# One pipeline of 64 turns in place of four stages, with the feed-forward in bursts inside the attention steps

## What is computed

```python
x = x + attention(layernorm(x), Wq, bq, Wk, bk, Wv, bv, Wo)      # scale 8**-0.5, corners of the scores set to -1e9
x = x + ffn(layernorm(x))
x = x + attention_b(layernorm(x), w_qkv, w_out)                  # no bias, scores / sqrt(128)
x = x + ffn(layernorm(x))

def ffn(x):
    gate = softmax(x.mean(axis=1) @ gate_w.T)                    # one gate vector per item
    top_w, top_i = top_k(gate, 2)
    top_w = top_w / (top_w.sum(-1) + 1e-8)
    h = gelu(einsum('bsd,bkcd->bksc', x, down_w[top_i]) + down_b[top_i]) * top_w
    return einsum('bksc,bkdc->bsd', h, up_w[top_i]) + (top_w * up_b[top_i]).sum(1)

```

## Time and profile before

| | |
|---|---|
| median of three runs | 1039.13 us (1038.06 to 1042.84) |
| the profiled execution | 1037.22 us |
| its span, first to last instruction | 1035.4 us |
| mean granted clock of TensorE | 0.968 |
| busy: PE, DVE, ACT, POOL | 88%, 76%, 73%, 57% |
| DMA | 131.64 MB, 127 GB/s |

### The profile page before, as it was taken

How to read it: one execution, slowest core, us unless ns; L and a number is a source line. 1 busy time by engine, 2 the same in 40 slices (tenths; PEclk the granted TensorE clock), 3 DMA queues, 4 the chain that set the end, 5 groups by cost and what they waited for, 6 DMA issues and landing times. The chain is left out here.

```text
span 1035.4 us, 27550 instructions
## 1 busy us (share of the span) xinstructions
PE 910.3 (88%) x10204; PEld 518.6 (50%) x10204; DVE 788.7 (76%) x1398; ACT 759.7 (73%) x1324; POOL 593.3 (57%) x1011
## 2 busy tenths in 40 slices
PE   1479999999999999984876999999999999998577
PEld 1235555555555555442653555555555555554266
DVE  0378888888888888843449898899999999885244
ACT  1147888888888888783753788888888888888566
POOL 4555666666666666423256566666666666643211
PEclk9989999999999999997997999999999999999889
DMA  8544545445554545300035444445544445440023
GB/s 235 173 147 146 145 145 147 145 147 145 145 148 145 145 146 147 113 3 21 2 103 161 154 148 149 150 144 150 149 154 147 145 144 152 148 130 3 1 60 105
DMA packets 140516, 131.64 MB, mean 127 GB/s; under 512 B 9880, under 2 KB 121888, under 8 KB 140256
## 3 DMA queue, kind: packets, MB, share of 16 engines
q1 hardware_dynamic: 139312, 128.49, 41.9%
q10 hardware_dynamic: 1072, 1.40, 0.5%
HBM read 73.75 MB, written 55.57 MB: 125 GB/s over the span
## 5 line engine op out<-in xcount | busy, mean ns | idle before, releaser
L379 DVE TENSOR_REDUCE nmax<-ring 128x4 f32<-128x1024 f32 x512 | 607.7, 1218 | 73.0 <-PE ring L504 73.0
L418 ACT ACTIVATE probs<-ring 128x1024 f32<-128x1024 f32 x512 | 509.1, 1024 | 78.8 <-PE ring L521 75.4
L486 PE MATMUL values_bank<-probs,values 128*32 128x256 f32 x4096 | 274.8, 386 | 5.8 <-ACT probs L418 5.8
L504 PE MATMUL ring<-k_stack,q_stack 64*128 64x256 bf16 x2048 | 201.2, 278 | 44.2 <-DMA k_stack<-scratch 20.4
L335 POOL TENSOR_SCALAR xy<-x,mv,rstd 128x128 f32<-128x128 f32 x256 | 201.1, 795 | 8.7
L521 PE MATMUL ring<-q_stack,k_stack 64*128 64x256 bf16 x2048 | 187.3, 273 | 0.4 <-DVE nmax L379 0.2
L486 PEld LDWEIGHTS values_bank<-probs,values 128*32 128x32 f32 x4096 | 107.0, 109 | 90.8 <-issue 24.0
L298 POOL TENSOR_SCALAR mparts<-nmax 128x32 bf16<-128x32 f32 x64 | 13.8, 216 | 231.7 <-DVE nmax L379 231.7
L504 PEld LDWEIGHTS ring<-k_stack,q_stack 64*128 64x128 bf16 x2048 | 75.6, 95 | 138.9 <-ACT probs L418 67.3
L521 PEld LDWEIGHTS ring<-q_stack,k_stack 64*128 64x128 bf16 x2048 | 83.8, 95 | 74.7 <-issue 37.8
L304 POOL TENSOR_TENSOR parts<-rest,parts 128x512 bf16<-128x512 f32 x64 | 74.1, 1158 | 5.4
(11 more groups left out here) (99 smaller groups left out, 1027.0 us busy)
## 6 DMA issues: line engine op xcount, KB each, us to landing
q_stack<-scratch SPq DMA_DIRECT2D x128, 256.0 KB
k_stack<-scratch SPq DMA_DIRECT2D x128, 256.0 KB
scratch<-parts SPq DMA_DIRECT2D x128, 192.0 KB, 2.3
scratch<-parts SPq DMA_DIRECT2D x128, 128.0 KB, 2.2
scratch<-parts SPq DMA_DIRECT2D x128, 64.0 KB, 3.1
out<-x SPq DMA_DIRECT2D x32, 128.0 KB, 1.8
q_stack<-maxT SPq DMA_DIRECT2D x128, 12.0 KB
scratch<-in_tail SPq DMA_DIRECT2D x8, 128.0 KB, 3.8
```

Source lines behind the costliest of these rows:

```text
L379: nc.vector.tensor_reduce(dst, src, axis=AX.X, op=ALU.max, negate=True).then_inc(max_done, 1)
L418: nc.scalar.activation(probs[g % 2][:, c:c + 2, :, :], pair_of_exps(n, p)[:, :, :].rearrange("p x (k q) -> p x k q", k=TILES), ACT.Exp).th ...
L486: last = nc.tensor.matmul(values_bank[32 * c:32 * (c + 1), a * TOKENS:(a + 1) * TOKENS], values[item % RING][:, k, PER_GROUP * g + c, :], ...
L504: last = nc.tensor.matmul(pair_of_scores(n, p)[:, a, t * TOKENS:(t + 1) * TOKENS], q_stack[z][rows, p, t * P:(t + 1) * P], k_stack[z][rows ...
```

## The change

The four stages and the blocks between them go. One pipeline runs over 64 turns, two per item: turn t is attention a of item t for t < 32, and attention b of item t - 32 from there. Steps run from n = -6 to 70. The feed-forward is done in 16 groups of four turns, each as a burst in one step (`BURSTS`): four first products (`down`) behind pair 4's scores, four Gelus on ACT behind the Exp of pair 3, the biases and second products (`up`) behind pair 4's Exp scores, two additions to x on DVE at position 5. The two products take a buffer each in the rotation of `ring`, which is now counted by a list of uses. Gating is done in ten batches of eight or four turns, each in three successive steps: logits, then weights and transposes, then biases, all in `m_bank` ahead of the value projection. DVE makes it, with ACT for Exp and the copies, and POOL for the split of the biases.

POOL copies both down weights of an item (`prepare`). Both halves of the scaled up weights are made by DVE at position 4, with one item in each of the four steps ahead of a burst for the first ten groups, two in each of the last two steps for the next four, and four in the step ahead for the last two. Gelu and Exp alternate on ACT, and no table is preloaded. The attention step's order on PE is changed: the value projection stands behind pair 4's scores, group 1's weighting behind pair 5's Exp scores, and the Exp scores of pair 6 behind the norm's transposes; ACT's copies of the values and of the norms move ahead by one position. In the opening nothing waits for a whole block: x is loaded in six pieces, of which four are issued in early steps, PE waits for three early weights, and POOL zeroes some more tiles. Results are stored two items at a time, one step behind their burst, in the second half.

```diff
-CHUNKS = ((0, 2), (2, 9), (9, ITEMS))
+CHUNKS = ((0, 2), (2, 9), (9, 15), (15, 21), (21, 27), (27, ITEMS))
+RING = 4
+TURNS = 2 * ITEMS
+GROUP = 4
+DEEP = 2 * GROUP
...
+        def sync_opening(sp):
+            load_x(sp, 0)
+            constant_rows(sp, 0)
+            load_x(sp, 1)
...
+            for dst, src in early:
+                act.dma_start(dst, src).then_inc(early_in, 16)
+            for dst, src in loads:
+                act.dma_start(dst, src).then_inc(consts_in, 16)
+            act.wait_ge(early_in, 16 * EARLY_LOADS)
+            nc.scalar.copy(identb[:, :], ident[:, :])
+            nc.scalar.mul(bqs[:, :], wa[:, 512:513], float(HEAD) ** -0.5)
+            nc.scalar.mul(wa[:, 0:WIDTH], wa[:, 0:WIDTH], float(HEAD) ** -0.5)
+            nc.scalar.mul(wb[:, 0:WIDTH], wb[:, 0:WIDTH], float(WIDTH) ** -0.5).then_inc(weights_ready, 1)
+            act.wait_ge(weights_ready, 1)
...
+        FIRST, LAST = -6, 70
+        BATCHES = ((0, 8), (8, 8), (16, 8), (24, 8), (32, 8), (40, 8), (48, 4), (52, 4), (56, 4), (60, 4))
+        LATE, FIRST_BY_VECTOR = 56, 0
+        BURSTS = (17, 21, 25, 29, 33, 37, 41, 45, 49, 53, 55, 57, 59, 63, 66, 70)
+        DOWN_AFTER, UP_AFTER = 3, 4
+        MIXING = 12
+        WHICH, NBEST = 3, 4
+        SPLITS = 5
+        PREPARED = {}
+        for group, burst in enumerate(BURSTS):
+            for j in range(GROUP):
+                turn = group * GROUP + j
+                early_step = burst - (1 if turn >= LATE else GROUP - j if turn < 40 else 2 - j // 2)
+                PREPARED.setdefault(early_step, []).append(turn)
...
+        def fill_pair(pe, *use):
+
+            if place[use] < 3:
+                return
+            kind, of, p = uses[place[use] - 3]
+            if kind == "scores":
+                pe.wait_ge(max_done, of * PAIRS + p + 1)
+            elif kind == "exps":
+                pe.wait_ge(exp_done, of * PAIRS + p + 1)
+            elif kind == "down":
+                pe.wait_ge(h_ready, (of + 1) * GROUP)
+            else:
+                pe.wait_ge(added, (of + 1) * 2)
...
+                    b = batch_at(n, 1)
+                    if b is not None:
+
+                        rows = BATCHES[b][1]
+                        sp.wait_ge(mixing, MIXING * b + WHICH)
+                        if before_batch(b):
+                            sp.wait_ge(wd_ready, before_batch(b))
+                            sp.wait_ge(wu_ready, before_batch(b))
+                        sp.dma_start(index[b % 2][0:1, 0:rows * TOP], which[0:rows, 0:TOP]).then_inc(index_in, 16)
+                    group = group_at(n - 1) if n <= LAST else None
+                    if group is not None and group * GROUP >= ITEMS:
+                        store(sp, group)
...
+                def prepare(turn):
+
+                    b, z, group = batch_of(turn), turn % DEEP, turn // GROUP
+                    if group not in experts:
+                        experts[group] = experts_of(group, pool)
+                    if turn >= DEEP:
+                        pool.wait_ge(up_done, (turn - DEEP) // 2 + 1)
+                    for k in range(TOP):
+                        last = nc.gpsimd.tensor_copy(wd[z][:, k:k + 1, :], down_sb[:, bass.ds(experts[group][TOP * (turn % GROUP) + k], 1), :])
+                    last.then_inc(wd_ready, 1)
...
+                def split_biases(b):
+
+                    parts_b, mid_rows, lo_rows = biasu_parts[b % 2], slice(ITEMS, 2 * ITEMS), slice(2 * ITEMS, 3 * ITEMS)
+                    pool.wait_ge(biases_ready, b + 1)
+                    if before_batch(b):
+                        pool.wait_ge(up_done, before_batch(b) // 2)
...
+                    if p == 3:
+                        for turn in PREPARED.get(n, ()):
+                            prepare(turn)
...
+                def best_of(b):
+
+                    rows = slice(0, BATCHES[b][1])
+                    dve.wait_ge(logits_done, b + 1)
+                    link(nc.vector.tensor_scalar(logit[rows, :], m_bank[rows, 0:EXPERTS], 1.0 / TOKENS, None, ALU.mult))
+                    link(nc.vector.max(best[rows, :], logit[rows, :]))
+                    if b > 0:
+                        dve.wait_ge(index_in, 16 * b)
...
+                    if p == 0 and batch_at(n, 1) is not None:
+                        weights_of(batch_at(n, 1))
...
+                    if p == 2 and batch_at(n, 1) is not None:
+                        spread(batch_at(n, 1))
...
+                    if p == 4 and batch_at(n, 0) is not None:
+                        best_of(batch_at(n, 0))
...
+                    if p == 5 and group_at(n) is not None:
+
+                        group = group_at(n)
+                        for half in range(2):
+                            dve.wait_ge(up_done, 2 * group + half + 1)
+                            xs = x[:, tiles_of(group * GROUP + 2 * half, 2), :]
+                            src = pair_of("up", group, 0)[:, half, :].rearrange("p (t d) -> p t d", d=WIDTH)
+                            nc.vector.tensor_tensor(xs, xs, src, ALU.add).then_inc(added, 1)
...
+                    if p == 4:
+                        for turn in PREPARED.get(n, ()):
+                            if turn >= FIRST_BY_VECTOR:
+                                if turn % GROUP == 0:
+                                    experts[0] = experts_of(turn // GROUP, dve)
+                                dve.wait_ge(weight_ready, batch_of(turn) + 1)
+                                if turn >= DEEP:
+                                    dve.wait_ge(up_done, (turn - DEEP) // 2 + 1)
+                                z, col = turn % DEEP, turn - BATCHES[batch_of(turn)][0]
+                                for k in range(TOP):
+                                    half = slice(HIDDEN * k, HIDDEN * (k + 1))
+                                    last = nc.vector.tensor_scalar(wu[z][half, :].unsqueeze(1),
+                                                                   up_sb[half, bass.ds(experts[0][TOP * (turn % GROUP) + k], 1), :],
+                                                                   weight[batch_of(turn) % 2][half, col:col + 1], None, ALU.mult)
+                                last.then_inc(wu_ready, 1)
...
+                    if p == 3 and group_at(n) is not None:
+
+                        group = group_at(n)
+                        act.wait_ge(biases_ready, batch_of(group * GROUP) + 1)
+                        for j in range(GROUP):
+                            turn = group * GROUP + j
+                            run, col = batch_of(turn) % 2, turn - BATCHES[batch_of(turn)][0]
+                            act.wait_ge(down_done, group * GROUP + 2 * (j // 2) + 2)
+                            if group > 0:
+                                act.wait_ge(up_done, 2 * (group - 1) + j // 2 + 1)
+                            src = pair_of("down", group, 0)[:, j // 2, (j % 2) * TOKENS:(j % 2 + 1) * TOKENS]
+                            nc.scalar.activation(hT[j][:, :], src, ACT.Gelu, bias=biasd[run][:, col:col + 1]).then_inc(h_ready, 1)
+                    if p == 3 and batch_at(n, 1) is not None:
+
+                        b = batch_at(n, 1)
+                        act.wait_ge(mixed_done, b + 1)
+                        if before_batch(b):
+                            act.wait_ge(wu_ready, before_batch(b))
+                        nc.scalar.copy(weight[b % 2][:, :], m_bank[:, 0:ITEMS])
+                        nc.scalar.copy(hotT[:, :, :].rearrange("p a b -> p (a b)"), m_bank[0:TOP * EXPERTS, ITEMS:5 * ITEMS]).then_inc(weight_ready, 1)
...
+                def down(group):
+
+                    fill_pair(pe, "down", group, 0)
+                    pe.wait_ge(wd_ready, (group + 1) * GROUP)
+                    bank = pair_of("down", group, 0)
+                    for j in range(GROUP):
+                        turn = group * GROUP + j
+                        nc.tensor.matmul(bank[:, j // 2, (j % 2) * TOKENS:(j % 2 + 1) * TOKENS],
+                                         wd[turn % DEEP][:, :, :].rearrange("p a b -> p (a b)"), normT[:, turn % ITEMS, :],
+                                         start=(j % 2 == 0), stop=(j % 2 == 1), skip_group_check=True).then_inc(down_done, 1)
...
+                def up(group):
+
+                    b = batch_of(group * GROUP)
+                    fill_pair(pe, "up", group, 0)
+                    pe.wait_ge(split_done, SPLITS * (b + 1))
+                    pe.wait_ge(wu_ready, (group + 1) * GROUP)
...
+                def mixes(b):
+
+                    fill_m(pe, weight_ready, b + 1)
+                    pe.wait_ge(mixing, MIXING * (b + 1))
+                    nc.tensor.transpose(m_bank[:, 0:ITEMS], wide[:, :, :].rearrange("p a b -> p (a b)"), ident[0:ITEMS, 0:ITEMS])
+                    for k in range(4):
+                        src = (hot if k == 0 else mix)[:, :, :].rearrange("p a b -> p (a b)")
```

(29 more changed lines are left out.)

1015 lines of the change are left out of this document (475 added, 540 removed).

## The result

The change makes the kernel slower: 1070.46 us, median of four executions (1069.75 to 1070.99), against 1038.6 us for the kernel before beside it. The ratio is 1.030, with an interval from 1.027 to 1.033. The forecast was 1022 us, with a range from 988 to 1056. The profiled execution took 1069.75 us. Its span is 1067.9 us, where the sum gave 1018.0, so 49.9 us have to be found.

The account below looks back on a forecast made before the run. PE's work and an equally long DVE-POOL-PE loop were taken to bound the 12.93 us step. Terms: 77.5 + 798.5 + 58.5 + 6.5 + 18 + 30 + 29 = 1018.0 us of span, forecast 1022 us, range 988 to 1056.

Parts of the forecast that it names:

- products: Scaled second weights made on DVE inside the steps: 18 us together, between 5 and 46.
- gating: Ten batches inside the attention steps, each over three successive steps: 30 us, between 18 and 48.
- 13 bursts: Feed-forward bursts in full steps: 4.5 us each, between 4.3 and 7.1, 58.5 us for thirteen.
- old work and step 63: Middle: 32 steady steps and the whole second stage, 798.5 us, plus the burst beside eight Exps, 6.5 us.
- The frame: First to last addition: 63 intervals, old work alone 798.5 us, steady step 12.93; PE's new order taken at nothing.
- Rival (c): Slower by the port or DVE loop: every product waits for POOL, 28 us more, 1050 us; chance 0.12.
- The expert numbers: DVE's load of eight per group: some 2 us, 0.85 beyond the reduction that it runs beside.
- the load at 6.43: Opening of the kernel before: ACT's 1.28 us table load ran ahead of a wait; bursts were taken to do likewise.
- Rival (b): Slower by table switches: both loads of every burst on the path, 7.1 us a burst, 1055 us; chance 0.15.
- rival (d): No difference: gating is 6 us a batch instead of 3.75, 1040 us; chance 0.14.
- Ends: First addition at 77.5, between 73 and 80; part after the last addition 29 us, between 25 and 36.
- rival (a): Nearly everything hides, steps follow PE's bare work: gating 18, preparation 5, bursts 4.3 each, about 988 us; chance 0.17.

Follow-up runs that it names:

- second kernel: The changed kernel with POOL instead of DVE making all scaled second weights: 1027.18 us, 1025.4 of span.
- e5_early_table: The changed kernel with products on POOL, plus the Gelu table load put by hand behind the Exp of pair 3: 1005.0 us of span.
- e9_read_first: e5_early_table plus DVE reading the logits ahead of the reduction of pair 4: 999.5 us of span; timed 1002.5 us, ratio 0.966.
- e10_table_alone: The changed kernel, products still on DVE, plus only the early Gelu table load: 1049.7 us of span.
- e11_early_timed: The same kernel as e5_early_table, timed over four executions: 1007.98 us, ratio 0.972 to the kernel before.
- e4_wait_order: The changed kernel with the two waits ahead of each Gelu in swapped order: 1066.2 us of span.

## Why the prediction was wrong

The second kernel gives the ledger of the middle: 913.6 us between first and last addition without products on DVE, 877.9 with one batch of gating, of which that batch is 6.5.

| term between first and last addition | forecast | measured | from |
|---|---|---|---|
| products | 18 | 46.7 | 960.3 - 913.6 |
| gating | 30 | 42.2 | 913.6 - 877.9, and the batch that stays |
| 13 bursts | 58.5 | 67.2 | 13 x (18.14 - 12.97) |
| old work and step 63 | 805.0 | 804.2 | the rest |
| sum | 911.5 | 960.3 | |

The ledger has no row for the clock, and the forecast of the middle had no term for it either. The changed kernel's middle has eight steps with a lower granted clock, each 1.2 to 1.6 us longer than the like step without, some 11 us together; the second kernel's has six, some 9 us; the two attention stages of the kernel before have none (granted clock 1.00 in both). So about 9 of the 42.2 us, and 2 or 3 of the 46.7, are clock. Without them gating is 33 us and the products about 44.

**The frame held.** 63 intervals of old work at the old period, the new order on PE at nothing: plain steps went from 12.93 to 12.97, and the rest of the ledger is within 1 us. That whatever stands between pair 4 and pair 7 on DVE lengthens the step held too, and it made the error below expensive.

**The products: wrong by 28.7 us, the step that failed.** I took "four of 17 were longer, by 0.6 us together" as the rate at which a product meets POOL. But that rate belonged to the place where the products stood, not to the operation. In the old feed-forward 4 of all 64 products were longer. At position 4 of a step without a burst POOL is in the split of queries and keys, L501 to L510. There a pair takes up to 1.88 us, not 0.58; in burst steps, where it comes later, it takes 0.58 (296.73). The trace of the kernel before showed this place already: in the step of the earlier trace rows, while DVE reduces pairs 4 and 5 from 199.51 on, POOL is in the same split.

```profile
200.10 0.62 POOL L302 TENSOR_SCALAR parts<-rest 128x512 bf16<-128x512 f32 x1
200.80 1.16 POOL L304 TENSOR_TENSOR parts<-rest,parts 128x512 bf16<-128x512 f32 x1
```

A product behind the reduction of pair 4 would have started near 200.7, beside these. The two-port lock that the Trainium skill states (SBUF — State Buffer, Who interferes with whom) would have said this; I named it, noted that by it most products would be delayed, and took the other value. The trace agrees with the rule in three ways: 564 ns in the mean with POOL beside about half of the products, 285 away from it, and statistics, which show no delay, at 286 in the same place. Rival (c) had the right cause, and its sum of 46 is close to the measured 46.7, but that is partly luck. It gave each of 104 products 0.31 us more, 32 us. In the trace 60 of the 128 products are long, by 0.6 us each in the mean (36 us), and the other 68 are not; 2 or 3 of the 46.7 are clock. Where a pair takes 1.2 to 1.3 us more, all of it passes to the step, but for the steps right behind a burst, which are only 0.8 to 0.9 longer. The forecast also counted the pairs beside gating and in bursts as free: those with logits cost 0.8 to 0.9 us of step, those in bursts without biases 0.7.

**The expert numbers: too small, and hidden.** I estimated 2 us for eight numbers. In the burst step 1.77 us of idle time stand behind the reduction of pair 4, which takes 1.23: 3 us in all, an estimate that takes the loads to start with the reduction, which no row shows. PE is in the first products meanwhile, and DVE's idle time before pair 5 was foreseen. As the burst step is the same without products but for 0.7 us (18.86 against 18.14), this cost is small.

**Bursts: wrong by 8.7 us.** The forecast rested on the load at 6.43, which ran ahead of a wait. In the bursts it runs behind the wait for the first products. The row at 6.43 stood in an opening where the load is the first thing that the block does, and it did not tell where a load goes once an operation of the other table stands before it. The text priced the other case at 1.1 us for PE; 1.15 was measured. Of the 5.17 us, 1.19 are this and 3.98 are the rest: so the product work itself was cheaper than my 4.3, of which 0.1 for two changes of form was an estimate that no run shows by itself. Rival (b), with both loads on the path and 7.1 us a burst, was wrong: the load back to Exp is hidden. The drain of 1380 ns that the Trainium skill gives beside each load (ScalarE: Activation LUTs, What ACT_TABLE_LOAD costs) is not seen here: the load at 294.84 ends at 296.12 and the Gelu starts at 296.13, the load at 298.06 starts 0.02 us after the copy before it has ended, and removing the loads after the early placement is worth 2.6 us of span, less than 0.1 per switch.

**Gating: wrong by 12.2 us, of which 9 are the clock.** Over eight batches, as the forecast and rival (d) count them, that is 5.3 us a batch, where I had 3.75 and rival (d) had 6; at the full clock it is 4.1. Logits cost 1.78 as against 1.4, the transposes 1.4 to 1.5 against 1.1, biases in a burst step 1.3 against 1.7. What I missed in the transposes is DVE: the small operations that build the one-hot rows stand ahead of pair 3 and of the scaled output `o`, and PE waits up to 1.3 us for `o` (L854, 7.4 us in nine waits). The clock drops of these two kernels all come in steps with transposes or biases (last section). The biases in a burst step wait for the Gelus and the table (L918 for `biasu`, 10.8 us in seven waits; 4.2 us once the load is early). I had foreseen this order, at 0.7 us.

**Ends.** First addition 2.4 us later than forecast, last part 1.2 us shorter. The last burst shows a term that was mis-sized there:

```profile
1057.14 2.88 DVE L648 TENSOR_SCALAR wu<-up_sb,weight 64x128 f32 x8 [3.08 <-issue]
...
1057.46 3.75 PE L812 MATMUL ring<-normT,wd 128*128 128x256 f32 x8 [1.11 <-POOL wd L428]
```

1.0 us was forecast for the first products beside the table load; the eight matmuls take 3.75 here, where the granted clock is 0.50, and 1.99 in the burst at 293.62. Shorter chains elsewhere in the end made up for it.

**What the prediction asked to look at.** Burst steps of 18.86 against a limit of 18.8, products of 564 ns instead of 270 to 300, and a table load that stands behind 1.35 us of idle time instead of right behind the operation before it, with nothing wrong in plain steps: so it pointed to the bursts and the products at once. The range failed because it was built from cases of which one is wrong at a time. Here three terms were off in the same direction (28.7 + 12.2 + 8.7 us), and they had something in common: each was taken from rows of a place where little ran beside the operation, and used for a place where much does. The sum of rival (a) was also slightly off: its terms give 983 us of span, which is 986.5 and not 988; this changes nothing here.

## What to carry to other kernels

A duration taken from a trace belongs to the place in which it was measured; before moving an operation, look at what the other engines run at its new place, POOL above all for a scale or copy on DVE. Where two functions alternate on ACT and the second one waits for a matmul, put its table load by hand ahead of that wait. Price the whole chain of a one-bank resource by who reads it: a read that stands behind a 1.2 us reduction costs PE that reduction. And before two single runs are compared by their totals, compare the granted clock step by step.

## What the runs showed of the hardware

**A DVE product beside POOL's split ends when a POOL instruction ends.** The row at 517.28 holds two products. The first takes 0.63 us and ends 0.08 us after POOL's first instruction (517.83), and the second takes 1.24 and ends 0.08 us after POOL's next one (519.08):

```profile
517.92 1.24 DVE L648 TENSOR_SCALAR wu<-up_sb,weight 64x128 f32 x1
```

So POOL started its next instruction between the two, and each product waited for one: 1.88 us for 0.57 of work. Of the 128 products of the changed kernel, 68 take 0.27 to 0.32 us, and all of the 60 longer ones end 0.06 to 0.11 us after a POOL instruction. The profile counts the wait as DVE's busy time, not as idle time. The product of the earlier trace rows also ended 0.08 us after POOL's instruction; it lost only 0.3 us because it had started 0.65 us into it. One row does not fit: in the kernel before, the product at 518.87 took 0.41 us and ended 0.28 us ahead of POOL's instruction, so not every POOL instruction holds one to its end.

**The clock drops after some of PE's waits.** A `mixes` step by stretches, first in `e5_early_table`, then the same step in `e9_read_first`:

```profile
786.11:802.20 16.09, 14.50 (x155) 7.38 (x153) 12.59 (x24) 10.67 (x20) 9.91 (x18) 0.89 0.38 118
```

```profile
781.82:796.16 14.34, 13.00 (x155) 6.88 (x153) 12.24 (x23) 10.70 (x20) 10.11 (x19) 1.00 0.42 131
```

The same matmuls take 14.50 us in one and 13.00 in the other. The mean granted clock of the first is 0.89: it fell from 2.4 GHz to 1.2 GHz for some 3.5 us (0.11 x 16.09 / 0.5), after PE had waited 1.15 us for `o` and 0.42 for `hotT`; in the second it had waited 0.84 and 0.42, and did not fall. A burst step with biases does the same in the changed kernel, where PE waited 1.74 us, and not in `e10_table_alone`, with the table loaded early, where it waited 0.55:

```profile
359.97 1.22 PE L918 MATMUL m_bank<-wa,xnT 128*128 128x128 f32 x4 [1.74 <-ACT biasu L721]
```

```profile
356.88 0.71 PE L919 MATMUL m_bank<-wa,xnT 128*128 128x128 f32 x4 [0.55 <-ACT biasu L722]
```

The one operation takes 1.22 us and the other 0.71. The step is 21.08 us and 18.24. So a step with a wait of about a microsecond on PE could take up to 1.5 us more than the wait explains, and the early table load gave back more than its own 1.15 us a burst. But one and the same step (36) of one and the same kernel took 15.74 us in `e5_early_table` and 14.35 in `e11_early_timed`, and step 29, with the same waits, 19.38 us in the changed kernel and 20.85 in `e4_wait_order`. So I can't say from these runs which waits bring the drop about; that stays open.
